# Moving the work between two chunks of a selective scan into its states, by borrowing a PSUM bank

## What is computed

```python
# 1: selective scan (N=16 states, R=64); h has a value per feature and state
x_dbl = einsum('bld,ed->ble', x, W_xproj)
delta_raw, Bm, Cm = split(x_dbl, [R, R + N], axis=-1)
delta = softplus(einsum('blr,dr->bld', delta_raw, W_dt) + b_dt)
dA = exp(einsum('bld,dn->bldn', delta, A)); dBx = einsum('bld,bln->bldn', delta * x, Bm)
h = dA_t * h + dBx_t ; y_t = einsum('bdn,bn->bd', h, C_t)      # over the tokens t
return y + x * D_param
# 2: FFN, 512 -> 2048 -> 512, with Hadamard transforms (folded into the weights by the kernel)
x = silu(x_gate) * x_up ; x = fwht(x * SU_dp) / SCALE ; x = x @ W_down.T * (Wscale_dp * SCALE)
# 3: mixer, 512 -> 1024 -> 512: gate silu(z), x through W_in and conv_w (folded), times D, W_out
# 4: mixture of experts: 64 experts, 8 per token, at most 128 tokens each
```

## Time and profile before

| | |
|---|---|
| median of 3 runs | 1922.38 us (1909.03 to 1934.32) |
| profiled execution | 1917.75 us, its span 1915.9 us |
| busy | PE 1547.9, DVE 1125.5, ACT 531.7, POOL 753.3 us |
| mean granted PE clock | 0.914 of 2.4 GHz |
| DMA | 380.29 MB, mean 198 GB/s |

### The profile page before, as it was taken

How to read it: one execution, slowest core, us unless ns; L and a number is a source line. 1 busy time by engine, 2 the same in 40 slices (tenths; PEclk the granted TensorE clock), 3 DMA queues, 4 the chain that set the end, 5 groups by cost and what they waited for, 6 DMA issues and landing times. The chain is left out here.

```text
span 1915.9 us, 18658 instructions
## 1 busy us (share of the span) xinstructions
PE 1547.9 (81%) x5792; PEld 1052.5 (55%) x5792; DVE 1125.5 (59%) x1693; ACT 531.7 (28%) x867; POOL 753.3 (39%) x452
## 2 busy tenths in 40 slices
PE   6967777677778688997798989999992188999993
PEld 3433333455566576775576777777881144555551
DVE  4866684599983899975899956444243122222220
ACT  3422221433323333323433312112110022223321
POOL 3255532065650445441345525672164422222222
PEclk9988898888889898999899999999995599999997
DMA  9655424289886354643354647996640299999997
GB/s 304 197 161 158 132 77 143 82 258 276 265 264 217 93 155 131 199 153 110 92 173 133 200 141 232 305 311 196 214 138 22 78 288 309 314 317 321 324 322 138
DMA packets 193530, 380.29 MB, mean 198 GB/s; under 512 B 20994, under 2 KB 95106, under 8 KB 192944
## 3 DMA queue, kind: packets, MB, share of 16 engines
q1 hardware_dynamic: 173424, 339.44, 56.6%
q0 software_dynamic: 20032, 39.92, 8.7%
HBM read 301.65 MB, written 124.35 MB: 222 GB/s over the span
## 5 line engine op out<-in xcount | busy, mean ns | idle before, releaser
L1056 POOL TENSOR_TENSOR y<-y,bx 128x2048 f32<-128x2048 f32 x64 | 293.5, 4585 | 290.3 <-DVE bx L915 290.3
L892 DVE TENSOR_TENSOR_SCAN bx<-bank,state,bx 128x512 f32<-128x512 f32 x256 | 311.1, 1265 | 3.6 <-ACT bank L703 2.3
L1062 POOL TENSOR_TENSOR act<-th,act 128x512 fp32r<-128x512 f32 x96 | 130.3, 1357 | 368.5 <-ACT act L639 368.0
L703 ACT ACTIVATE bank<-dl,an 128x512 f32<-128x512 f32 x256 | 175.3, 690 | 338.0 <-DVE bx L892 337.9
L458 PE MATMUL bank<-xn2T,ring 128*128 128x512 f32 x576 | 242.3, 421 | 16.3 <-DVE xall L805 12.9
L459 PE MATMUL bank<-xn2T,ring 128*128 128x512 f32 x576 | 235.6, 409 | 0.0
L460 PE MATMUL bank<-xn2T,ring 128*128 128x512 f32 x576 | 235.2, 408 | 0.0
L469 PE MATMUL bank<-ring,act 128*128 128x512 f32 x384 | 158.4, 412 | 31.4 <-DVE th L794 31.4
L1229 PE MATMUL bank<-wgu,xeT 128*128 128x384 f32 x512 | 177.5, 490 | 0.0
L470 PE MATMUL bank<-ring,act 128*128 128x512 f32 x384 | 155.6, 405 | 0.0
L471 PE MATMUL bank<-ring,act 128*128 128x512 f32 x384 | 155.2, 404 | 0.0
(11 more groups left out here) (139 smaller groups left out, 2301.7 us busy)
## 6 DMA issues: line engine op xcount, KB each, us to landing
ring<-w_all SPq DMA_DIRECT2D x288, 512.0 KB
wgu<-wgu_in SPq DMA_DIRECT2D x64, 768.0 KB
wde<-wd_in SPq DMA_DIRECT2D x64, 384.0 KB, 9.6
slots<-empty_in SPq DMA_DIRECT2D x16, 1154.0 KB, 9.0
xe<-slots SPq DMA_DIRECT2D x64, 288.5 KB
w_all<-staged_u SPq DMA_DIRECT2D x64, 256.0 KB, 2.8
w_all<-fst SPq DMA_DIRECT2D x48, 256.0 KB, 3.4
w_all<-staged_d SPq DMA_DIRECT2D x32, 256.0 KB, 3.1
```

The source lines that it names most:

```text
L703: nc.scalar.activation(dA[k % 2][:, :], dl[:, k, :], ACT.Exp, scale=an[:, k, n:n + 1]).then_inc(S_dA, 1)
L892: nc.vector.tensor_tensor_scan(b[:, k, :], dA[k % 2][:, :], b[:, k, :], state[:, k, n:n + 1], ALU.mult, ALU.add).then_inc(S_sc, 1)
L1056: nc.gpsimd.tensor_tensor(y[:, :, :], y[:, :, :], bx[n % 2][:, :, :], ALU.add).then_inc(S_ya, 1)
```

## The change

The head and tail disappear. A position count of 5 stands once, at the start (`HEAD`), and a chunk is its 16 states of 4 positions (`SPAN = 4 * NS`).

- The steps between two chunks run inside the states. Bank 1 (`PC`), which holds C's broadcast from position 1 to the product with C, is lent in positions 0 and 1 of a state to one step each (`borrow_at`): in chunk c, states 1 and 2 transpose y of chunk c-1, states 3 and 4 its second norm, states 5 and 6 the first norm of chunk c+1, state 7 its product with W_xproj, states 9 to 12 its four products with W_dt, states 15 and 0 the mixer's norm of chunk c-1. PE waits at each for the previous product with C, and for the step before it to be read.
- The broadcast of C moves behind the quanta of position 1.
- Softplus: Relu and Abs, Exp per block on ACT; the correction per block and the last sum on POOL (new tiles `spr`, `spc`); the rounding stays on DVE.
- `y`, `dl` and `xdr` get two buffers. `bx` has one; the product with C is written to a new tile `hc`, which POOL adds. The column of the state is saved by ACT.
- Order of halves: ffn 0, ffn 1 and mixer of each chunk in turn. 48 quanta of chunk c-1's FFN stand from state 5 to position 0 of state 14 of chunk c, the 24 of the mixer of c-2 from position 2 of state 0 to the end of state 4. The drain holds mixer 2, both halves of ffn 3, then mixer 3 alone; all 12 routed tiles stand beside the first three of them.
- winx and conv share memory with the preparation and are loaded when it ends. Folds stand in states 12 to 15 of chunk 0 and 1 to 4 of chunk 1. The 16 stores of plain mixer weights come each 1.5 positions from state 5 of chunk 1, the 16 fills of `slots` each 6 positions from its state 8.
- The statistics of chunk 0 are computed behind the constants.

```diff
-HALVES = [("ffn", 0, 0), ("ffn", 0, 1), ("ffn", 1, 0), ("mixer", 0, 0), ("ffn", 1, 1), ("ffn", 2, 0), ("mixer", 1, 0), ("ffn", 2, 1),
-          ("ffn", 3, 0), ("ffn", 3, 1), ("mixer", 2, 0), ("mixer", 3, 0)]
+HALVES = [(kind, c, part) for c in range(NCH) for kind, part in (("ffn", 0), ("ffn", 1), ("mixer", 0))]
...
+            HEAD = 5
+            SPAN = 4 * NS
+            state_at = lambda c, n, m: HEAD + SPAN * c + 4 * n + m
+            DRAIN = HEAD + SPAN * NCH
...
+            for c in range(1, NCH):
+                first = PER * half_of["ffn", c - 1, 0]
+                if c >= 2:
+                    spread(quanta[first - PER:first], range(state_at(c, 0, 2), state_at(c, 5, 0)))
+                spread(quanta[first:first + 2 * PER], range(state_at(c, 5, 0), state_at(c, 14, 1)))
+            spread(quanta[-4 * PER:-PER], range(DRAIN + 2, DRAIN + 2 + 3 * PER))
+            spread(quanta[-PER:], range(DRAIN + 6 + 3 * PER, DRAIN + 6 + 4 * PER))
...
+                        borrow_at[state_at(c, 1 + t // 2, t % 2)] = ("yT", c - 1, t)
+                        borrow_at[state_at(c, 3 + t // 2, t % 2)] = ("ffn_T", c - 1, t)
...
                     def bcast_c(c, n):
-                        wait(pe, S_cm, NS * c + n if n else 0)
+                        for m in (1, 0):
+                            if state_at(c, n, m) in borrow_at:
+                                pe.wait_ge(*returned(*borrow_at[state_at(c, n, m)]))
+                                break
+                        wait(pe, S_cm, NS * c + n)
...
+                            borrowed(c, n, 0)
                             side(state_at(c, n, 0))
+                            borrowed(c, n, 1)
                             side(state_at(c, n, 1))
+                            bcast_c(c, n)
...
+                            if (n, m) in ((2, 3), (3, 2)):
+                                for t in ((0, 1) if n == 2 else (2, 3)):
+                                    wait(dve, n3.tp, TT * (c - 1))
+                                    normed(n2, c - 1, t, xall[:, c - 1])
+                            if (n, m) == (14, 1):
+                                mixer_stats(c - 1)
...
+                            if n + 1 == NS and c + 1 < NCH:
+                                dve.wait_ge(S_bm, i + 1)
+                                delta_x(c + 1)
+                            dve.wait_ge(S_cb, i + 1)
+                            dve.wait_ge(S_sc, KT * (i + 1))
+                            wait(dve, S_ya, i)
+                            nc.vector.tensor_tensor(hc[:, :, :], bx[:, :, :], PC[:, :].unsqueeze(1).to_broadcast([P, KT, CH]),
                                                     ALU.mult).then_inc(S_cm, 1)
...
+                    def correction(c, k):
+                        pool.wait_ge(S_rs, KT * c + k + 1)
+                        pool.wait_ge(S_rel, KT * c + k + 1)
+                        nc.gpsimd.tensor_tensor(spc[:, k % 2, :], dl[c % 2][:, k, :], spc[:, k % 2, :], ALU.subtract).then_inc(S_co, 1)
+                        pool.wait_ge(S_co, KT * c + k + 1)
+                        nc.gpsimd.tensor_tensor(spr[:, k, :], spr[:, k, :], spc[:, k % 2, :], ALU.add).then_inc(S_sp, 1)
```

## The result

The change makes the kernel slower by 0.9%: 1934.84 us (median of 20 runs, 1915.44 to 1944.71) against 1918.18 us (20 runs of the kernel before beside them, 1903.53 to 1939.17), a ratio of 1.009 with a 95% interval of 1.0061 to 1.0118. The forecast was 1.3% less. The number lies in the stated range (1855 to 1945), the sign is the other one. The profiled execution has a span of 1937.6 us at a mean granted clock of 0.904.

What follows compares the result with a forecast made beforehand. VectorE bounded chunks 1 to 3's states, latency chains the gaps, PE chunk 0 and the drain. Stages reached 1412.4 us; with the 478.9 tail the span is 1891.3, scaled to 1898, 1.3% less; range 1855 to 1945.

Steps and rivals of the forecast that it cites:

- I let VectorE be first at nine: Eleven norms behind the product with C, chunks 1 to 3: at nine VectorE starts before GpSimd's add and does not wait.
- rival (b): At those nine norms GpSimd's add starts first, each norm waits some 4.1 us: +37, 1935 us; chance 0.12.
- Start, +12: Up to the first state: statistics behind the constants delay norm and delta products; first state at 61.0, not 48.65 us.
- Chunk 0, +15: Chunk 0's states: transposes and delta products 3.5, late winx and conv loads 9, delta x 2.3 us.
- The serial chain: States 1 to 4 of chunk 1: PE borrows the bank before folding, 14.3 us a state; 62 with norms, plus 4.8.
- 4 us for DMA: Chunk 1's 48 quanta: 16 plain stores, once per 1.5 positions, lie on ring loads and add 4 us.
- Between the chunks, 33: Stretches without quanta, inside states 14 to 0: VectorE's own list is the path, PE idle 33 us.
- 228 and 215: Loaded stretches of chunks 2 and 3: PE is the bound, 227.7 and 215 us.
- only states 2 and 3 would be longer: Chunks 2 and 3: only these states have VectorE above PE's sum, +4 us.
- 318 said: Drain: last transposes and mixer 3 standing alone behind ffn 3 add 22 us to 296, making 318.
- (a): Whole kernel: loads, folds, DMA, VectorE, norms and routing stalls are all absorbed, 42 us less, 1856; chance 0.24.
- (c): Loaded states: waits at borrows bring the low clock, 567 us become 667; whole time 1998 us, slower; chance 0.12.

Runs made afterwards that it cites:

- both tiles ahead: Changed kernel with the normed tile pairs of states 2, 4 and 14 moved ahead of the product with C; 1900.98 us, ratio 0.9934 to the kernel before.
- the run with all four edits: Changed kernel plus normed tiles ahead of the product with C, statistics ahead of the constants, plain weights every two positions, folds moved; 1865.99 us, ratio 0.9747.
- the run with the low parts on VectorE: Changed kernel with the 16 low parts of the plain mixer weights made on VectorE, one position earlier, instead of GpSimd; 1936.02 us, ratio 1.0106.
- the run with one tile ahead: Changed kernel with one normed tile of each of the three pairs ahead of the product with C, one directly behind; 1901.26 us, ratio 0.9949.

## Why the prediction was wrong, point by point

**The step that failed** is "I let VectorE be first at nine". It counted eleven places behind a product with C as one norm each and priced each at nothing or 4.1 us by who is first. At eight of the eleven two tiles stand, and the two have different answers: the first tile was ahead of the add by 0.16 us, as I had assumed (but for the two places behind a gate/up pair), and the second, 0.5 us later, behind it. I had the two rows needed, the durations of tile and add, but never laid the second tile's start beside the add's. Forecast for all holds in chunks 1 to 3: 5.6 us (two places at 2.8). Measured: eight places, 31 us in tile time and 33 in states, of 46 us over in all. With them gone the kernel ran at 0.9934 of the kernel before: the sign of the forecast, half of its size (1.3%); the other half are the terms below, the loads of the plain weights above all. The rival (b) named the hold, but by a condition that was not met (at all nine of its places VectorE was first, and what was held there was a second tile that it did not count). That its 1935 is the measured 1934.84 is luck: holds account for some 27 us over the forecast, other terms for the rest. The row that the rival cites for the hold also bears on its tie: in the earlier trace rows the tile starts at 1317.32, 0.03 us ahead of the subtraction, and is held all the same, so a lead of hundredths was not enough. The Trainium skill ("SBUF — State Buffer", Who interferes with whom) says that whoever issues first has the shared pair for the whole instruction; by that rule each instruction has to be placed against the add by itself. The trace agrees where the tile's lead is 0.15 us or more, and the earlier trace rows shows that for smaller ones the order of the recorded starts does not tell.

**Start, +12.** Right in the hold of the last two tiles; undoing the order gave 9.6 back. The forecast's 61.0 is a wrong sum: its own terms (42, 8.3, 2.6, 3.2, 4.6, 2.3) give 63.0, and 63.3 was measured. That nearness is in part luck: the last Exp ended at 46.9, not 50.3, but GpSimd's eight corrections, one behind the other from 42.4 on, ended only at 53.0, where the forecast had two behind the last Exp.

**Chunk 0, +15.** Measured 20.2. The wait for winx was 8.09 us (9 said). Missed: the statistics of chunk 1, which now stand in state 3 (2.9 us, VectorE 14.6 of 16.1), and, in state 4, a held tile (3.24 instead of 0.54 us). States 9 and 10 took 2.7 and 1.6 us more than before, state 12 10.7 more.

**Chunk 1.** The serial chain was priced at 62 + 4.8 for states 1 to 4; it took 79.6. Of the 13 over, 8 are the two holds, 3 the folds' low clock (7.9 over four folds instead of 4.8). For the 48 quanta I had 4 us for DMA "on ring loads". The loads that were late were not the ring's but those of the plain weights, and who waited was ScalarE: 8 us came back when they were spaced.

**Between the chunks, 33.** 36.6; with both tiles ahead 32.5. The sum by VectorE's list was right to half a microsecond, but for the held tile. The last stretch, 25.4 forecast, took 31.9 and without the hold still 27.8; where those 2.4 us come from was not looked for.

**Chunks 2 and 3.** PE is the bound, as said; 228 and 215 against 223.8 and 212.0 in the run with all four edits. That only states 2 and 3 would be longer than PE's sum was wrong for the changed kernel: the hold in state 4 of chunk 2 cost 4.2 us there and passed 2.6 on to state 5, though PE was busy 16.8 of 17.1 us.

**Drain and tail.** 318 said, 315.0 measured; the gap ahead of mixer 3 was 13.3 us (12 said). The tail, the same code, was 2.9 us longer here, less than it varies.

**The other rivals.** (a), all absorbed, did not come: the waits for winx, the folds at the low clock and the holds were there. (c), the low clock in the loaded states: the granted clock was 0.96 to 0.98 in them.

## What to carry to other kernels

Where two instructions on VectorE that can be held by GpSimd follow each other behind the instruction that also releases a long GpSimd one, the first slipped through here and the second waited for all of it: place each on the time line by itself, and put both ahead of the releaser. A wait for "VectorE" at PE can come from a load in a third engine's queue; follow it back through every in-order queue before moving work. And a wait that leaves one engine comes back in the queue of whoever reads its result: moving the folds of chunk 1 behind the broadcast made VectorE wait 19.9 instead of 15.1 us for them; reading them later took 13.3 us off the four states, of which 7.5 were left at the last quantum.

## What the runs showed of the hardware

**Which VectorE instructions are held.** A normed tile (one SBUF input, 0.54 us) was held, and so was a subtraction of two SBUF tiles, from 0.67 to 2.26 us, when it came in the middle of an add; the same subtraction 0.16 us ahead of an add took 0.69 (L919, in the run with the low parts on VectorE; L1182 is the add there):

```profile
479.63 4.58 POOL L1182 TENSOR_TENSOR y<-y,hc 128x2048 f32<-128x2048 f32 x1
...
480.31 2.28 DVE L1026 TENSOR_TENSOR bx<-u,bank 128x2048 f32<-128x2048 f32 x1
...
482.50 2.26 DVE L919 TENSOR_TENSOR fst<-praw,fst 128x512 fp32r<-128x512 f32 x1
```

The product with B, which reads a PSUM bank and one SBUF tile, was not (2.28 us, the same as alone), nor were the statistics, which ran in the changed kernel beside an add at 0.68 us a tile:

```profile
683.19 2.47 DVE L852 BATCH_NORM_STATS2 n_st<-xall 128x6 f32<-128x512 f32 x4
683.35 4.62 POOL L1173 TENSOR_TENSOR y<-y,hc 128x2048 f32<-128x2048 f32 x1 [1.08 <-DVE hc L1044]
```

The Trainium skill ("SBUF — State Buffer", Who interferes with whom) draws the line there: by it two SBUF inputs, or the fast mode that `tensor_scalar` can enter, contend with GpSimd, and one SBUF input outside it does not; these rows agree.

**How small a lead decides.** In the twelve profiles a normed tile whose start is recorded 0.15 to 0.50 us ahead of a GpSimd instruction always took 0.54 or 0.55 us. The two recorded only 0.02 and 0.03 us ahead, both in the drain of the kernel before, took 1.60 and 1.59; none lies between. A tile that was first delays the add a little in turn: the adds beside one took 4.73 to 4.87 us in the changed kernel and the run with one tile ahead, those beside no normed tile at most 4.64.

**GpSimd lets go between two instructions.** At the start the third tile waited for the end of the scaling (23.20) and then ran, to 23.48, while the butterfly behind it started at 23.27; the fourth waited for that one. Wherever one was held, the tile ended 0.28 us behind the GpSimd instruction, whether another GpSimd one stood behind it or not.

**The tail varies.** Behind the last quantum the same instructions took 454.0 us in one profile and 488.2 in another of twelve (DMA share 0.85 and 0.86), more than most edits here are worth.
